# Adapted gated feed-forward with routed experts: some copies, one load and some reduction steps take other places in the written-out order

## The reference, cut to what matters

```python
# x: 8 x 256 x 1024, seen as 2048 tokens; one adapter per sequence
def lora_add(base, inp, A, B):                      # rank 16, scale 0.5
    Ab, Bb = A[layer_idx][lora_indices], B[layer_idx][lora_indices]
    return base + einsum('bor,bnr->bno', Bb, einsum('bri,bni->bnr', Ab, inp)) * 0.5
gate = lora_add(x @ W_gate.T, x, A_gate, B_gate)    # 1024 -> 2752
up   = lora_add(x @ W_up.T,   x, A_up,   B_up)
act  = silu(gate) * up
y    = lora_add(act @ W_down.T, act, A_down, B_down)    # 2752 -> 1024
logits = y @ Wg + bg                                # 8 experts
_, top_idx = top_k(logits, 2)
z = relu(einsum('bsd,edh->bseh', y, W_e) + b_e)     # of each token, its two experts
return x + take_along_axis(z, top_idx[..., None], axis=2).mean(axis=2)
```

## Time and profile before

| | us |
|---|---|
| median of 3 runs | 1841.7 |
| lowest and highest | 1838.97, 1843.03 |
| the profiled execution | 1838.5 |
| its span, first to last instruction | 1836.6 |
| TensorE busy in the span | 1808.3 |
| VectorE, GpSimd, ScalarE busy | 1255.6, 1097.3, 754.8 |

### The profile page before, as it was taken

How to read it: one execution, slowest core, us unless ns; L and a number is a source line. 1 busy time by engine, 2 the same in 40 slices (tenths; PEclk the granted TensorE clock), 3 DMA queues, 4 the chain that set the end, 5 groups by cost and what they waited for, 6 DMA issues and landing times. The chain is left out here.

```text
span 1836.6 us, 25207 instructions
## 1 busy us (share of the span) xinstructions
PE 1808.3 (98%) x8578; PEld 1505.3 (82%) x8578; DVE 1255.6 (68%) x1489; ACT 754.8 (41%) x1197; POOL 1097.3 (60%) x712
## 2 busy tenths in 40 slices
PE   8999999999999999999999999999999999999997
PEld 6788888888888888888888888888888888888886
DVE  7977887885567797888888886477798743234400
ACT  5544444443543335444443444443323333333332
POOL 3788888873444454446656543444434777777674
PEclk9999999999999999999999999999999999999999
DMA  6466566645577655555566565576635875567653
GB/s 227 161 232 222 207 205 224 240 138 172 194 247 245 220 186 169 189 179 180 189 205 210 187 205 191 192 255 221 223 109 188 246 195 149 145 188 194 150 104 48
DMA packets 128973, 350.34 MB, mean 191 GB/s; under 512 B 15296, under 2 KB 17216, under 8 KB 128576
## 3 DMA queue, kind: packets, MB, share of 16 engines
q1 hardware_dynamic: 110608, 286.92, 45.6%
q0 software_dynamic: 17952, 61.75, 14.1%
q10 hardware_dynamic: 288, 0.02, 0.0%
HBM read 267.49 MB, written 90.05 MB: 195 GB/s over the span
## 5 line engine op out<-in xcount | busy, mean ns | idle before, releaser
L1831 PE MATMUL PS<-R,ring 128*128 128x512 f32 (+1 forms) x1804 | 708.5, 393 | 11.0 <-DVE R L1022 8.4
L1832 PE MATMUL PS<-R,ring 128*128 128x512 f32 (+1 forms) x1804 | 704.0, 390 | 0.0
L1833 PE MATMUL PS<-R,ring 128*128 128x512 f32 (+1 forms) x1804 | 703.5, 390 | 0.0
L1831 PEld LDWEIGHTS PS<-R,ring 128*128 128x128 f32 x1804 | 339.7, 188 | 79.2 <-DVE ring L956 11.6
L1833 PEld LDWEIGHTS PS<-R,ring 128*128 128x128 f32 x1804 | 339.3, 188 | 71.8
L1832 PEld LDWEIGHTS PS<-R,ring 128*128 128x128 f32 x1804 | 339.8, 188 | 66.0
L824 POOL TENSOR_TENSOR ring<-raw,ring 128x1024 fp32r<-128x1024 f32 x78 | 192.2, 2464 | 268.9 <-ACT ring L963 268.8
L803 POOL DMA_INDIRECT brw<-in_bgu,idx_b x88 | 100.4, 1141 | 222.6 <-DVE R L1139 184.9
L1831 PE MATMUL PS<-ring,R 128*128 128x512 f32 x592 | 231.7, 391 | 1.7 <-DVE FT L1323 1.7
L1832 PE MATMUL PS<-ring,R 128*128 128x512 f32 x592 | 230.8, 390 | 0.0
L1833 PE MATMUL PS<-ring,R 128*128 128x512 f32 x592 | 230.4, 389 | 0.0
(11 more groups left out here) (192 smaller groups left out, 2391.0 us busy)
## 6 DMA issues: line engine op xcount, KB each, us to landing
raw<-in_wp SPq DMA_DIRECT2D x122, 512.0 KB, 4.4
act_scratch<-FT SPq DMA_DIRECT2D x140, 256.0 KB, 4.9
FT<-act_scratch SPq DMA_DIRECT2D x70, 512.0 KB, 3.9
raw<-in_we SPq DMA_DIRECT2D x64, 512.0 KB, 5.6
ytp<-in_wgb SPq DMA_DIRECT2D x96, 256.0 KB, 4.7
raw<-wt_scratch SPq DMA_DIRECT2D x40, 512.0 KB, 4.4
out<-in_xn SPq DMA_DIRECT2D x17, 512.0 KB, 5.5
y_scratch<-FT SPq DMA_DIRECT2D x7, 1024.0 KB, 5.9
```

The lines of the kernel that those rows point to most:

```text
L1831: e.matmul(out_, hi, whi, start=start, stop=False, skip_group_check=True)
L1832: e.matmul(out_, hi, wlo, start=False, stop=False, skip_group_check=True)
L1833: return e.matmul(out_, lo, whi, start=False, stop=stop, skip_group_check=True)
```

## The change

Five keys change. The copies `a_hi` of the first two act tiles of a group move by one operation, behind both copies of the last adapter factors; their `a_lo` keep their places relative to other work. `d_hi` of the first piece goes behind `e_copy` k=3 of unit 20. `b_hi` of (t, w) = (0, 0) goes behind one `w_hi` and behind `e_copy` k=3 of the odd unit before it; on VectorE, in group 1, its `b_lo` goes behind one `l_step1`, and for p = 10 also behind `l_sum(1)` and `choice(1)`. `load_y` of tile 4 goes ahead of `act_store(1, 4)`; for the other tiles the order stays. The logits' steps 0 to 31 go five to two pieces instead of two to one, so that they end at piece 22 and not 25; their `load_wb` move with them, `load_wb` 3 to 9 going past `load` or `load_a` jobs of SyncE.

```diff
         def l_key(g, o):
 
             if o < 32:
-                m = 10 + o // 2
+                m = 10 + 2 * o // 5
...
             if k % 8 == 0:
-                sp.add(l1_key(k - 1) + 0.5, load_y, k // 8)
+                sp.add(l1_key(k - 1) + 0.35, load_y, k // 8)
...
             for m in range(NM):
-                act.add(op_m(g, m) - 3.97, d_hi, g, m)
+                act.add(op_m(g, m) - (3.97 if m else 3.9), d_hi, g, m)
...
                 if jj < 3:
-                    key = op(g, [144.2, 144.3, 149.4][jj])
+                    key = op(g, [145.2, 145.3, 149.4][jj])
...
                         else:
-                            key = op(g, 14 * p) + [[-1.6, 4.3], [0.1, 4.3]][t][w]
+                            key = op(g, 14 * p) + [[-0.93, 4.3], [0.1, 4.3]][t][w]
```

## The result

| | before | after |
|---|---|---|
| median of 8 runs each, us | 1841.07 | 1834.66 |
| lowest and highest | 1838.97, 1843.03 | 1832.44, 1838.77 |
| the profiled execution | 1838.5 | 1832.44 |
| its span | 1836.6 | 1830.6 |

The ratio of the times is 0.9969, with a 95% interval of 0.9958 to 0.998. The kernel is faster by 6.4 us of medians, where 5.4 was forecast, and 1834.66 lies in the range given.

The account below looks back on a forecast made before the run. TensorE was taken to bound the kernel, busy 1808.3 of 1836.6 us, so only its waits could be regained. Gains 2.0 + 2.2 + 1.2 = 5.4 us off the median 1841.7 gave 1836.3 us, range 1832 to 1840.

Parts of the forecast that it names:

- Part 1: `b_hi` behind `w_hi` and `e_copy` k=3: removes TensorE's breaks at odd units of the first group, 2.0 us.
- The three excesses: Time over 0.88 us of six L1877 at three odd units, first group: 1.29, 0.35 and 0.31 us.
- I count the other odd units at nothing: Odd units of the first group beyond the three with a break read were taken to gain nothing.
- The upper bound: Cost if `b_hi` lost its cover of two products: 1.2 us at each of 20 units, 24 us; excluded.
- Part 2: `a_hi` behind `b_hi`, `d_hi` behind `e_copy`: closes the L1877 breaks at unit 20, both groups, 1.09 + 1.08, 2.2 us.
- Part 3: The y load of tile 4 ahead of seven act stores: removes two TensorE waits near 933, 1.2 us.
- The other term: 0.35 us for a second wait on the late y tile, beside 0.85 at 933.82, within the 1.2 us.
- Part 4: Logits' steps 0 to 31 at 2.5 to a piece, pieces 10 to 22: no TensorE wait there, 0 us.
- Part 3 paid back: Rival: late stores hold `c_add(11, 0)` and the 1.2 us return as another wait; 1837.5 us, chance 0.12.
- Part 2 lost: Rival: a tile or factor lands later, or another wait takes the 2.2 us at unit 20; 1838.5, chance 0.13.
- Crowding: Slower rival: three steps in a piece, one held 2.2 us by GpSimd's split, fill VectorE; 1865 us, chance 0.04.
- TensorE's waits for L1194 gone from the list: Sign expected in the changed profile: no TensorE wait for the ScalarE copy L1194 remains.

Follow-up runs that it names:

- part 3 alone: Only the y load of tile 4 moved ahead of the act stores, on the kernel before; 1837.38 us.
- the adds ahead: The kernel after with the adds (L1323) of stages 2, 3 and 5 put ahead of the logits' steps; median 1832.55 us, ratio to before 0.9957.

## Why the prediction was right, point by point

**What bounds the kernel.** Right: every gain of the three parts is a closed gap of TensorE, nearly all at places that were named, and no stretch outside them changed by a cause that the experiments tie to the change.

**Part 1, forecast 2.0.** The mechanism held: with only this part, 2.23 us. The three excesses that were added up are 1.95; the other 0.28 were small breaks in units 7, 9 and 11 of the same execution, which were counted at nothing. The size is that of the one execution read. The gaps come from a gather's landing and scatter with it: in the five other profiles without part 1 the same L1877 blocks lost 2.6, 2.75, 3.7, 2.8 and 3.8 us over 0.88 each, 3.1 on the mean of the five. So the term was sized too low for the median, by about 1 us, and "I count the other odd units at nothing" is the step that failed: four of the five had a break of 0.65 to 0.93 us in unit 15, which was clean in the execution read. With 3.1 the three parts would make 7.1 us; the medians give 6.4, with an interval of 3.7 to 7.7. The upper bound, a `b_hi` too late for its own use, never came: in no profile does TensorE wait at `product(2p, 1)`. Its waits for L1139, 0.16 to 0.40 us in five profiles, stand at other uses, in kernels with and without part 1.

**Part 2, forecast 2.2.** Measured 1.21 + 1.33 = 2.54. The breaks closed as worked out (1.97 to 0.88 us); the 0.12 and 0.25 over it are a late start of the two blocks, which a reading of the block's own length leaves out. The act tile did not land late.

**Part 3, forecast 1.2.** Measured 1.49, in each of the eight profiles that have it. The idle time in the brackets is less than what a wait costs: from 932.58 to 933.82 there are 1.24 us, 1.01 more than a step of 0.23, where the bracket has 0.85. The other term was misread. The 1.2 us of the earlier trace rows are the 0.85 and a wait of 0.32 at 77.44, in unit 2 of group 0, which part 3 doesn't touch and which the kernel after still has. Unit 11 had its second delay at 936.90: 0.50 us after the matmul before it, a break of 0.27 that is too short for the list, and 0.08 at the next matmul. That this comes to 0.35 as well is luck. The landing was taken at 5.1 us from the issue and was 3.1 (922.16 to 925.26). The stores ahead make the difference: this load took 5.0 to 5.5 us in the six profiles with the old order and 2.9 to 3.1 in the eight with the new one. The Trainium skill, page "DMA: Bandwidth & Descriptors", in its table of fixed and variable cost, makes it 2.6 by estimate for this tile; but that table is for transfers that GpSimd issues, and this one is SyncE's, so its figure only stands beside the 3.1 of the trace. It decided nothing. The delayed stores and the row of step 33 (at 931.50, 1.34 us idle) reached nobody, as argued.

**Part 4, forecast 0.** Right in its value: 23.61 us of VectorE in the window of 27 that the earlier trace rows shows, where 23.4 was worked out, and nothing measurable in the time. The reason was too simple. "No wait of TensorE lies in these pieces" holds for the profile of before, and not for every execution: a late d tile makes one at s3, with two steps to a piece too.

**The rivals.** Part 3 paid back: fell, by the kernel with part 3 alone. Part 2 lost: fell. Crowding: the mechanism is true and comes in by doses. Its forecast was that held steps eat up VectorE's idle time until the factors are late, from 9 held steps in 13 pieces. Four steps to a piece showed that the bound is nearer: three held steps in the pieces of s2 are enough, since the add that frees a bank stands behind them in VectorE's order, long before all slack is used. So the deciding point named was the wrong one. The price with four steps to a piece was 5.7 to 5.9 us in each group; the rival's own case, a held step in each of 13 pieces for 14.2 us, never came up. The Trainium skill, page "SBUF — State Buffer", the section on two separate sides, has the shared port locked for a whole instruction. The trace agrees: the held steps, 2.87 to 2.89 us for 0.68, get to their work when the split has ended. They are not "as long as the split", as the prediction says: the one at 607.30 took 2.87 us beside a split of 2.49, and ended 0.55 us after it.

**What was not foreseen.** The 1.16 us in unit 0 of group 1 and the 1.0 gained at the start nearly cancel in the one profile after. The second is the granted clock's and not the change's; the first is a landing's scatter but for the 0.3 us that stay open. Without them and the end the three parts are 6.26 us; the medians differ by 6.4. "TensorE's waits for L1194 gone from the list" did not come true as it stands: the one in unit 2 of group 0 stays.

**Left open.** What makes the gather land 5.7 us after its issue at one time and 6.9 at another, and the d tile late in some executions, was not tried. Nor was the kernel with the adds ahead told from the kernel after.

## What to carry to other kernels

In a written-out order, look for a copy that TensorE needs and that stands behind a job waiting for a DMA: the gap scatters with the landing from one execution to the next, so its worth is a mean over several profiles, and it is read from start to start, not from the idle time in brackets. When two moves repair the same late copy, their gains don't add; test each alone. Before reductions are packed more densely beside GpSimd's work, look at which job stands behind them in VectorE's order and frees a bank: try that job first in the order, since one held reduction in each piece delays it long before VectorE is full, and then see where the wait has moved. Before a stretch at the start of an execution is counted as gain, compare the moment at which the granted clock rises.

## What the runs showed of the hardware that was not expected

After some stalls of TensorE in the middle of dense work the granted clock fell to 1.2 GHz and came back after some 3.4 us: after waits of 1.80 us (144.44), 1.68 us (1404.45), 3.83 and 4.03 us. Matmuls then start 0.43 us apart for 0.23, so that such a wait costs 1.6 to 1.7 us more than itself. It does not follow each such stall: the 1.95 us wait at 685.35 was not followed by it, nor was the 1.7 us wait of the expert part in the other 13 profiles, and none of the waits of 1.52 us or less was. So closing a wait of near 2 us can be worth nearly twice its length, in some executions. At the start the rise of the clock scatters too: the first 25 matmuls took from 6.97 to 8.21 us over the 14 profiles.
